# Attention and feed-forward block in split f32: turning the probabilities with block transposes and transfers instead of on TensorE

## The reference

```python
x = L0_attn_x                                  # 2 x 1024 x 512, f32
xn = layernorm(x)
q, k = rmsnorm(xn @ Wq.T, q_norm_w), rmsnorm(xn @ Wk.T, k_norm_w)   # 32 query heads, 8 key heads, 128 each
scores = q @ k.T / sqrt(128) + slope[head] * (pos_k - pos_q), masked above the diagonal
s = (softmax(scores) @ v) @ Wo.T
g = silu((silu(x @ w_gate.T) * (x @ w_up.T)) @ w_down.T)            # inner size 1376; its input is xn
return x + s * g
```

## Time and profile before

| | |
|---|---|
| median of 3 runs | 2455.03 us |
| the profiled execution | 2455.46 us |
| its span, first to last instruction | 2453.7 us |
| PE busy | 2422.6 us, 99% |
| VectorE busy | 1693.7 us, 69% |
| ScalarE busy | 1236.1 us, 50% |
| GpSimd busy | 756.9 us, 31% |
| DMA, share of 16 engines | 10.5% |

### The profile page before, as it was taken

How to read it: one execution, slowest core, us unless ns; L and a number is a source line. 1 busy time by engine, 2 the same in 40 slices (tenths; PEclk the granted TensorE clock), 3 DMA queues, 4 the chain that set the end, 5 groups by cost and what they waited for, 6 DMA issues and landing times.

```text
span 2453.7 us, 37432 instructions
## 1 busy us (share of the span) xinstructions
PE 2422.6 (99%) x13232; PEld 2070.7 (84%) x13232; DVE 1693.7 (69%) x3788; ACT 1236.1 (50%) x2548; POOL 756.9 (31%) x2053
## 2 busy tenths in 40 slices
PE   7999999999999999999999999999999999999998
PEld 6888888888888888878888888888888888888887
DVE  7777777777778787823377787777777777777132
ACT  4555554555545555543355555555555545545333
POOL 2323231413233323244522232323232314131443
PEclk9999999999999999999999999999999999999999
DMA  3010000000000000023320101010000000010232
GB/s 130 1 40 4 27 18 27 18 27 18 27 18 27 18 27 18 27 91 125 112 78 1 44 1 44 1 44 1 27 18 26 18 27 18 1 44 14 90 103 103
DMA packets 23289, 92.19 MB, mean 38 GB/s; under 512 B 6592, under 2 KB 6720, under 8 KB 19136
## 3 DMA queue, kind: packets, MB, share of 16 engines
q1 hardware_dynamic: 23104, 89.80, 10.5%
HBM read 85.60 MB, written 4.19 MB: 37 GB/s over the span
## 4 chain that ended last, share of the span: by engine, by line
PE 96%; DVE 2%; ACT 1%; issue 1%; POOL 0%; DMA 0%; DVEq 0%; ACTq 0%; POOLq 0%
PE out_ps L401 17%; PE score_ps L377 16%; PE out_ps L414 14%; PE qkv_ps L351 14%; PE ring_ps L388 10%; PE qkv_ps L352 7%; PE score_ps L504 5%; PE qkv_ps L504 4%; PE ring_ps L520 4%; PE ring_ps L359 2%; PE out_ps L520 1%; PE ring_ps L364 1%; PE score_ps L351 0%; DVE y L997 0%; DVE xT_lo L868 0%
## 5 line engine op out<-in xcount | busy, mean ns | idle before, releaser
L597 ACT ACTIVATE pT_hi<-ring_ps 128x512 fp32r<-128x512 f32 x576 | 344.0, 599 | 509.8 <-PE ring_ps L388 497.2
L818 DVE TENSOR_TENSOR pT_lo<-ring_ps,pT_hi 128x512 fp32r<-128x512 f32 x576 | 396.8, 690 | 90.6 <-ACT pT_hi L597 86.0
L589 ACT ACTIVATE probs<-probs,low_min 128x896 f32<-128x896 f32 (+7 forms) x512 | 395.2, 774 | 50.4 <-DVE low_min L810 50.1
L1016 POOL TENSOR_SCALAR rs_x<-sq_sum 128x5 f32<-128x5 f32 x122 | 24.8, 203 | 1128.1 <-DVE sq_sum L749 1128.1
L388 PE MATMUL ring_ps<-ident,probs 128*128 128x128 f32 x2304 | 345.6, 273 | 0.0
L388 PEld LDWEIGHTS ring_ps<-ident,probs 128*128 128x128 f32 x2304 | 281.7, 140 | 42.1
L810 DVE CUSTOM_DVE_ANT_0 probs<-score_ps,rel_sb,slope 128x512 f32<-128x512 f32 (+5 forms) x504 | 301.7, 599 | 5.7 <-PE score_ps L377 4.3
L377 PE MATMUL score_ps<-kv_hi,qT_hi 128*128 128x320 f32 (+4 forms) x760 | 275.6, 363 | 3.0 <-DVE xT_lo L868 2.0
L401 PE MATMUL out_ps<-pT_hi,kv_hi 128*128 128x512 f32 x576 | 265.8, 461 | 2.9 <-DVE pT_lo L818 2.6
L377 PE MATMUL score_ps<-kv_hi,qT_lo 128*128 128x320 f32 (+4 forms) x760 | 261.0, 343 | 0.0
L377 PE MATMUL score_ps<-kv_lo,qT_hi 128*128 128x320 f32 (+4 forms) x760 | 260.3, 342 | 0.0
(11 more groups left out here) (178 smaller groups left out, 5293.5 us busy)
## 6 DMA issues: line engine op xcount, KB each, us to landing
qkv_raw<-w_ffn_dram SPq DMA_DIRECT2D x44, 768.0 KB, 4.2
qkv_raw<-w_qkv_dram SPq DMA_DIRECT2D x15, 1536.0 KB, 6.9
o_raw<-w_o_dram SPq DMA_DIRECT2D x16, 1024.0 KB, 4.8
o_raw<-x_dram SPq DMA_DIRECT2D x4, 1024.0 KB, 6.7
out_dram<-y SPq DMA_DIRECT2D x16, 256.0 KB, 3.7
probs<-x_dram SPq DMA_DIRECT2D x3, 1024.0 KB, 7.9
qkv_raw<-w_qkv_dram SPq DMA_DIRECT2D x4, 384.0 KB, 6.6
probs<-x_dram SPq DMA_DIRECT2D x2, 512.0 KB, 4.8
```

Source lines behind the costliest of these rows:

```text
L589: act.activation(row, row, ACT.Exp, scale=-1.0, bias=low_min[:, i % 2, h, HEAD_CHUNKS[i] - 1:HEAD_CHUNKS[i]], accum_out=row_sum[:, i % 2, ...
L597: act.activation(pT_hi[:, n % SLOTS, :], ring_ps[:, ring_bank(r), :], ACT.Copy).then_inc(ring_high, 1)
L818: dve.tensor_tensor(out=pT_lo[:, n % SLOTS, :], in0=ring_ps[:, ring_bank(r), :], in1=pT_hi[:, n % SLOTS, :].bitcast(F32), op=ALU.subtract) ...
```

## The change

The probabilities are no longer transposed on PE.

- `bias` writes the probabilities of all four heads so that 32-column squares of the heads lie side by side (`by_head`, `by_chunk`), the same bytes seen in two ways. After `exp`, VectorE transposes each 32 x 32 square in place (`turn_blocks`, one instruction for each head and tile). SP then moves the squares to their partitions with 16 transfers for each tile, SBUF to SBUF (`turn_probs` on SP, 512-byte runs), straight into the place of the low halves, pT_lo, which grows from 4 to 15 slots. ScalarE makes the high half from there, VectorE writes the low half over it.
- The probabilities are not divided. The reciprocals of the row sums go out to DRAM (`rec_away`, issued ahead of the 16 transfers) and come back broadcast to all partitions (`rec_home`, behind them), and VectorE multiplies them into the attention (`scale_att`), whose halves are then made from SBUF.
- Weighing follows the scores two steps later instead of one (LAG = 2), out_project three. Scores, weighing and out_project are no longer interleaved: a step on PE is projection, transposes of q and k, out_project, all scores, all weighing. In the batch's first unit and behind its last step the order is adapted.
- The squares for q and k are five activations with accumulators on ScalarE (`squares`); the reduction on VectorE goes away. The projection alternates between two pairs of banks, into which q and k are also transposed. Scores have three banks instead of two.
- Slopes and inverse slopes are loaded once for all units. The feed-forward weights have two slots instead of three.

```diff
+BLOCKS, SQUARE = 4, 32
+HIGH_SLOTS = 4
...
-        probs = [sb("probs0", [P, G, S - P]), sb("probs1", [P, G, S])]
-        pT_hi, pT_lo = sb("pT_hi", [P, SLOTS, G * P], F32R), sb("pT_lo", [P, SLOTS, G * P], F32R)
+        probs = [sb("probs0", [P, G * S]), sb("probs1", [P, G * S])]
+        pT_hi, pT_lo = sb("pT_hi", [P, HIGH_SLOTS, G * P], F32R), sb("pT_lo", [P, HOMES, G * P], F32R)
...
+            def rec_away(U, i):
...
+                alone(rec_done, t)
...
+                sp.dma_start(rec_out_at[slot].rearrange("g p -> p g"), rec[:, i % 2, :], allow_slow_non_contiguous=True).then_inc(rec_out, 16)
+            def turn_probs(U, i):
...
+                alone(probs_turned, t * G)
+                if t > 2:
+                    alone(weighed, homes_free(U, i))
...
+                for a in range(BLOCKS):
+                    for k in range(BLOCKS):
+                        b = (a + k) % BLOCKS
+                        sp.dma_start(homes[b * SQUARE:(b + 1) * SQUARE, :, a], by_chunk[i % 2][a * SQUARE:(a + 1) * SQUARE, 0:i + 1, b]
+                                     ).then_inc(probs_back[t % 2], 16)
+            def rec_home(U, i):
...
+                alone(rec_out, t * 16)
+                if t > 2:
+                    alone(att_split, t - 2)
+                sp.dma_start(att[i % 2][:, :], rec_out_at[slot:slot + 1].rearrange("a g p -> a (g p)").to_broadcast([P, G * P])
+                             ).then_inc(rec_back[slot], 16)
```

PE's step:

```diff
+            def step(U, i, first, last):
+                if not (last and i >= TILES - 2):
+                    project(U + (i + 2) // TILES, (i + 2) % TILES, first and i + 2 < TILES)
+                if not (last and i >= TILES - 1):
+                    turn_qk(U + (i + 1) // TILES, (i + 1) % TILES, first and i + 1 < TILES)
...
+                if not (first and i <= LAG):
+                    out_project(U, i)
+                for k in range(sooner, chunks):
+                    scores(U, i, k, first)
...
+                    for j in range(p + 1):
+                        weigh(V, p, j, None if first and i == LAG else U * TILES + i - LAG)
```

ScalarE's squares and, below the line of dots, its step:

```diff
+                for h in range(G + 1):
+                    ins = act.activation(qk[i % 2][:, h * P:(h + 1) * P], acc[:, h * P:(h + 1) * P], ACT.Square,
+                                         accum_out=sq_sum[:, i % 2, h:h + 1])
...
+                    highs = [] if i >= TILES + LAG or first and i < LAG else list(range(p + 1))
+                    for j in highs[:HIGH_SLOTS]:
+                        high_probs(V, p, j)
...
+                        for h in range(G - 1):
+                            exp(U, i, h)
+                        for j in highs[:1]:
+                            high_probs(V, p, j)
+                        highs = highs[1:]
+                        exp(U, i, G - 1)
...
+                    for j in highs:
+                        high_probs(V, p, j)
```

VectorE's block transposes, low halves, scaling of the attention, and its step:

```diff
+            def turn_blocks(U, i, h):
+                dve.wait_ge(exped, (tile(U, i) - 1) * G + h + 1)
+                row = by_head[i % 2][:, h, 0:(i + 1) * BLOCKS, :]
+                dve.transpose(row, row).then_inc(probs_turned, 1)
...
+                dve.tensor_tensor(out=home(i, j), in0=home(i, j).bitcast(F32), in1=pT_hi[:, n % HIGH_SLOTS, :].bitcast(F32),
+                                  op=ALU.subtract).then_inc(probs_low, 1)
...
+                dve.tensor_tensor(out=scaled, in0=out_ps[:, :].rearrange("p (a g n) -> p g a n", g=G, a=BLOCKS), in1=scaled,
+                                  op=ALU.mult).then_inc(att_scaled, 1)
...
+                def step(U, i, first, last):
+                    if not (first and i <= LAG):
+                        scale_att(U, i)
+                    N, n = U + (i + 1) // TILES, (i + 1) % TILES
+                    if not (last and i >= TILES - 1) and not (first and i == 0):
+                        scale_qk(N, n, first and n)
+                    V, p = U - (i < LAG), (i - LAG) % TILES
+                    lows = [] if i >= TILES + LAG or first and i < LAG else list(range(p + 1))
+                    for j in lows[:1]:
+                        low_probs(V, p, j)
+                    if not (first and i <= LAG):
+                        low_att(U, i)
+                    for j in lows[1:HIGH_SLOTS]:
+                        low_probs(V, p, j)
+                    lows = lows[HIGH_SLOTS:]
...
+                        low_q(N, n, first and n)
+                        if n:
+                            low_k(N, n, first)
...
+                        add_y(U, i, first)
+                    for k in range(sooner, chunks):
+                        bias(U, i, k)
+                        h, part = divmod(k, HEAD_CHUNKS[i])
+                        if part == HEAD_CHUNKS[i] - 1 and h >= 2:
+                            turn_blocks(U, i, h - 2)
...
+                        for h in (G - 2, G - 1):
+                            for j in lows[:1]:
+                                low_probs(V, p, j)
+                            lows = lows[1:]
+                            if h == G - 1:
+                                reciprocals(U, i)
+                            turn_blocks(U, i, h)
+                    for j in lows:
+                        low_probs(V, p, j)
```

711 lines of the change are left out of this document (310 added, 401 removed).

## The result

The changed kernel takes 2511.74 us (median of 4 runs, 2509.57 to 2520.47), the kernel before 2455.38 in the same session. The ratio is 1.0236 (95% interval 1.0211 to 1.0260): slower by 56 us, where the prediction had it 102 faster. The profiled execution took 2520.47 us with a span of 2518.7, against 2453.7 before. The forecast for the span was 2453.7 - 117 + 15 = 2352, so 167 us are to be explained. The profiled execution is the slowest of the four, 9 us over the median, so what is read from its span comes out some 10 us larger than by the medians.

What follows compares the result with a forecast made beforehand. PE was taken as the bound, VectorE nearly binding: a unit 112.3 + 6.0 + 2.0 = 120.3 us, 7.3 less than before. Over 16 units, 2455 - 117 + 15 = 2353 us, range 2235 to 2560.

Steps and rivals of the forecast that it cites:

- step 2: Third step of a unit on PE, forecast at 10.5 us of PE work.
- the sum of 112.2 for PE alone: PE's work over steps 0 to 7 of one attention unit without the probability transposes: 112.2 us.
- Price of a block transpose: VectorE's added transposes: one cycle a column, 21.4 us a unit, a 1024-wide one near 1.2 us.
- rival C: VectorE's block transpose takes two cycles a column, 17.5 us more a unit: 2633 us; chance 0.12.
- VectorE's load: VectorE's work in one attention unit after the change: 105.0 us, 94% of PE's 112.3.
- GpSimd's hits: Low halves on VectorE delayed by GpSimd's subtractions of w_o and w_qkv in steps 3 and 6: 2.0 us a unit.
- the rule: VectorE instructions with two SBUF inputs share a read port with GpSimd; whoever comes second waits for the whole instruction.
- part 3: PE and VectorE waiting on each other, with ScalarE's lateness, from out_project to out_project: 6.0 us of waits a unit.
- part 4: The 16 SBUF-to-SBUF transfers a tile: 5.2 us of issuing, tile 7 7.2 us of packets, all covered; cost nothing.
- part 5: Filling and draining the longer pipeline at batch starts and ends: 3 us each start, 5 each end, about 15 in all.
- D: Step 1 of each unit: at 87 ns a packet tile 7 lands 9.7 us late; 12.8 a unit, 2558 us; chance 0.16.
- E: Waits in a unit, from ScalarE's order and GpSimd's interference, reach 12 to 17 us: 2405 to 2490 us; chance 0.14.

Runs made afterwards that it cites:

- the best version: Against the run with GpSimd low halves in steps 6-7 and two transposes between biases: step 1's high and low halves queued later; 2413.17 us, ratio 0.9832.

## Why the prediction was wrong, point by point

- **PE.** Right. The step that nothing disturbs, step 2, was forecast at 10.5 us and takes 10.3 or 10.4 in every run; the sum of 112.2 for PE alone was never reached, but some run comes within 0.6 us of it in each step except 6 and 7.
- **Price of a block transpose.** Right, and rival C falls: 1233 ns at 1024 columns ("near 1.2"), 301 at 128, so 1.04 ns a column. The column means are those of the earlier trace rows.

```profile
L785 DVE STREAM_TRANSPOSE probs<-probs 128x1024 f32<-128x1024 f32 x64 | 78.9, 1233 | 0.0
...
L785 DVE STREAM_TRANSPOSE probs<-probs 128x128 f32<-128x128 f32 x64 | 19.1, 301 | 0.3
```

  The Trainium skill's 311 ns (VectorE: DVE Perf Modes, section The three transpose paths) is for bf16 at 128 columns; here f32 takes 301.
- **VectorE's load.** Right: 103.2 us a unit against 105.0. One term was added up wrongly: 32 divides from 285 to 750 ns, less 0.08 each, are 14.0 us and not 12.0, so the sum should have been 103.0.
- **GpSimd's hits.** Put at 2.0 us a unit and nearly nothing in the kernel after: the 576 low halves last 692 ns in the mean, 685 in the median, 1162 at most. That is the order's doing and not the rule's: with low_att first, low_att itself lasts about 1 us longer in each of steps 3 and 6.
- **The loop through both engines (part 3).** Wrong, and as large as the transfers. The hand count gave 6.0 us of waits a unit, transposes included, and 2.0 for GpSimd. The run without transposes and with one transfer has 5.6 already; with the transposes and one transfer it is 11.3 (123.5 - 112.2). So the load was right (103.2 of 112.2 is 92%, forecast 94%) and what follows from it was not. Steps 6 and 7 were put at 0.4 and 1.6 over PE, with a share of 1.1 for the hand-overs, and are at 2.3 and 4.0. The point of the hand count that failed is when VectorE reaches the late low halves. Counted from the end of out_project, the last one of step 7 was to be done at 10.9 us and is done at 12.6, that of step 6 at 8.3 and is done at 9.2, in each of the 12 units. Step 7's 1.7 us are a hand-over of 0.2 from PE, add_y at 0.79 instead of 0.6, eight biases at 0.76 instead of 0.70, and low_k with its wait, 0.7, which stands in front of the late low halves and is not in the count at all. The high halves were there: 1.5 us or more ahead of each late low half. Unit 3, VectorE and then ScalarE:

```profile
543.34 0.35 DVE L757 SCALAR_TENSOR_TENSOR kv_lo<-even_ps,wcol,kv_hi 128x128 fp32r<-128x128 f32 x1 [0.41 <-ACT kv_hi L555]
...
545.37 0.65 DVE L797 TENSOR_TENSOR pT_lo<-pT_lo,pT_hi 128x512 fp32r<-128x512 f32 x1
```
```profile
543.21 0.62 ACT L570 ACTIVATE pT_hi<-pT_lo 128x512 fp32r<-128x512 f32 x1
```

  PE, due at the last block of step 7 at 9.3 us, starts it at 12.6: 3.3 late, where 1.6 were forecast. ScalarE's order counts only once GpSimd makes these low halves: step 7 is 20.4 us then, and 18.4 with two high halves ahead of the last exponential.
- **Transfers (part 4).** Wrong; "the transfers cost nothing" fails in two terms. The issue on SP was taken from a plain load, 0.328 us; these take 0.603 in the median, at least 0.507, so 16 take 10 us or more, against 5.2. Tile 1 has only step 2 to cover it, 10.4 us, and I looked at the cover of tiles 6 and 7 alone, since their packets are most. The packet of 512 B was put at 28 ns, which tile 0 has (27), and takes 38 in the median but 63 in the mean in tile 7, 16.2 us instead of 7.2. Tile 7 is there 18.6 us after the first issue instead of 9.5, with 14 us of cover. Together 61 us: 28 for the issues, 33 for the packets or for the crossing of partitions.
- **What is queued behind the wait.** Not in the prediction, though its own method asks for it. Part 3 lists "one low half 0.6, low_att 0.65" in that order and gives the low half no wait for the transfer. Putting low_att first gives 55 us. These are no third part beside the 61: it is the same lateness, kept from reaching PE.
- **The clock.** Not in the prediction. The mean granted clock of the execution is 0.96; with two levels, 1.2 and 2.4 GHz, that is (1 - 0.96) x 2 x 2518.7 = 201 us at 1.2 GHz, against 10 before. About half of it lies in the 12 units, half at the ends of the batches. Three windows of PE alone around the end of step 7 (length, PE busy, clock, DMA share, GB/s), and matmuls of the projection at the lower level and at the higher:

```profile
541.00:544.00 3.00, 1.03 (x5) 1.00 0.00 1
544.00:546.70 2.70, 1.59 (x6) 1.00 0.00 0
546.70:549.50 2.80, 2.80 (x11) 0.52 0.35 57
```
```profile
547.57 0.63 PE L364 MATMUL even_ps<-qkv_lo,xT_hi 128*128 128x512 f32 x1
548.00 0.41 PE L365 MATMUL even_ps<-qkv_lo,xT_hi 128*128 128x256 f32 x1
548.21 0.63 PE L364 MATMUL even_ps<-qkv_hi,xT_lo 128*128 128x512 f32 x1
```
```profile
591.98 0.40 PE L364 MATMUL qkv_ps<-qkv_lo,xT_hi 128*128 128x512 f32 x1
592.22 0.28 PE L365 MATMUL qkv_ps<-qkv_lo,xT_hi 128*128 128x256 f32 x1
592.34 0.40 PE L364 MATMUL qkv_ps<-qkv_hi,xT_lo 128*128 128x512 f32 x1
```

  A pair takes 0.64 us instead of 0.36. After waits that left PE busy 2.6 of 5.7 us the clock fell, and the work behind them took 1.8 times as long. So a wait is paid for twice. 8.1 us of a unit are at the lower level; were PE busy through all of them, that would be 8.1 x (1 - 0.36 / 0.64) = 3.5 us, an upper end. It is part of the effects above, not an addition: the run without transposes and with one transfer has a clock of 0.987.
- **Ends of the batches (part 5).** Direction right, size wrong: outside the 12 units the kernel after takes 59 us more than before, and 72 more than forecast (15 of fill and drain, less 7.3 for each of four units). One transfer takes 19 of them away, no transposes 32, both 44. What is left beside these two is 936 us where 908 were forecast: if those four units gain what was forecast, filling and draining the longer pipeline costs 43 us and not 15. What was missed is also that transposes and transfers have no projection to hide behind there. At the start of the second batch ScalarE waits 5.10 and 7.03 us for a transfer, in a stretch of 47 us in which PE is busy 30.
- **The sum of the miss.** In the profiles' spans, by the run with one transfer: transfers 76 us (56 in the 12 units, 19 at the ends), the loop 12 x 5.3 = 64, less 24 for GpSimd's hits that did not come, and the ends 53: 169, against the 167. By the medians the transfers are 61; the two profiles are the slowest run of the one kernel and the fastest of the other. The split depends on the order of removal, since each wait hides part of another: without the block transposes the transfers cost 3.5 us a unit and not 4.7.
- **The rivals.** D had the sign, and the place (step 1 of each unit, ScalarE's first high half of tile 7) that part 4 denied; its price of 87 ns a packet was too high and its blindness to the issues left out step 3. E had its waits of 12 to 17 us a unit (16.0 measured), but none of its reasons. The case that came is late transfers and the loop at once, and the prediction priced them only one at a time.

What stays open: how the 5 us a unit that the best version has over PE alone outside steps 1 and 4 split between ScalarE's order, the long low_att in steps 3 and 6, and GpSimd's low halves of w_qkv, for which PE also waits at the start of step 6; why the transfers stall for a few us at a time; and whether the 33 us are the packets' size or the crossing of partitions.

## What to carry to other kernels

When a step's work is moved to an engine or a queue with time to spare, ask of every instruction that first waits for it what stands behind it in its engine's fixed order; here one subtraction's place was worth 55 us, as much as the transfers themselves. Count a string of small transfers by its issues and compare it with the shortest step in front of its use, not with the mean. And where a second engine comes to 94% of the first, a unit takes longer than the work of either: here the waits were a tenth of it, and PE's clock fell behind them.
